# Attention stage: keys projected once and repeated through DRAM, 96-row operands, row maxima of batch 0 in the key bank

## What is computed

```python
B, S, D, H, HD = 32, 128, 128, 16, 8
q = split_heads(layernorm(x) @ Wq.T + bq)      # [B, H, S, HD]
k = split_heads(ctx @ Wk.T + bk)
v = split_heads(ctx @ Wv.T + bv)
scores = einsum('bhqd,bhkd->bhqk', q, k) / sqrt(HD)
attn = softmax(where(mask, finfo.min, scores), axis=-1)
x = x + tanh(g_xattn) * (merge(attn @ v) @ Wo.T + bo)
x = x + tanh(g_ffn) * ffn(layernorm(x))        # 8 experts, 512 hidden, thresholded softmax gate
```

## Time and profile before

| | us |
|---|---|
| median of 3 runs | 677.84 (677.28 to 678.39) |
| the profiled execution, its own time | 676.37 |
| its span, first to last instruction | 674.4 |
| PE busy | 635.5 (94%) |
| DVE busy | 544.5 (81%) |
| ACT busy | 433.8 (64%) |
| POOL busy | 185.6 (28%) |

### The profile page before, as it was taken

One profiled execution on the slowest core, in us unless ns is written; L12 is line 12 of the kernel. 1 busy time (PEld: TensorE's weight loads), 2 busy tenths in 40 slices (PEclk: granted clock), 3 DMA queues, 4 the chain that ended last, 5 costly groups with the idle time before them and its releaser, 6 DMA issues.

```text
span 674.4 us, 14486 instructions
## 1 busy us (share of the span) xinstructions
PE 635.5 (94%) x3964; PEld 483.3 (72%) x3964; DVE 544.5 (81%) x1085; ACT 433.8 (64%) x764; POOL 185.6 (28%) x240
## 2 busy tenths in 40 slices
PE   3999999999999999739999999999999999999998
PEld 2666666766666666427878878878788788787886
DVE  5778888998898888545888888888888888888886
ACT  3466666666666666417766766767667667666673
POOL 6224444444444442200121221221212212212121
PEclk9999999999999999958999999999999999999999
DMA  6544344444444444103112112111111111121110
GB/s 190 141 121 123 106 119 120 117 113 114 118 114 113 113 106 106 58 0 71 48 48 63 47 48 64 47 47 62 47 49 60 47 62 47 47 62 47 46 63 17
DMA packets 37402, 52.74 MB, mean 78 GB/s; under 512 B 9344, under 2 KB 20480, under 8 KB 37376
## 3 DMA queue, kind: packets, MB, share of 16 engines
q1 hardware_dynamic: 37376, 52.42, 28.4%
HBM read 26.58 MB, written 2.23 MB: 43 GB/s over the span
## 4 chain that ended last, share of the span: by engine, by line
PE 85%; DVE 6%; DMA 3%; SPq 2%; issue 2%; ACT 2%; POOL 0%; DVEq 0%; ACTq 0%; POOLq 0%
PE ps_h L1081 9%; PE ps_y L1061 9%; PE ps_y L1063 9%; PE ps_y L1062 9%; PE ps_h L1083 9%; PE ps_h L1082 9%; PE scores L1014 5%; PE scores L1015 4%; PE scores L1022 3%; PE scores L1023 3%; DVE neg_max L659 3%; PE heads L1033 3%; PE misc L902 2%; PE misc L903 2%; PE misc L904 2%; PE misc L888 2%
## 5 line engine op out<-in xcount | busy, mean ns | idle before, releaser
L632 ACT ACTIVATE h_sb<-ps_h,b_sb 128x512 f32<-128x512 f32 x256 | 175.9, 688 | 109.2 <-PE ps_h L1083 95.7
L846 DVE TENSOR_TENSOR h_low<-h_sb,h_high 128x512 fp32r<-128x512 f32 x256 | 164.4, 682 | 0.0
L842 DVE CAST h_high<-h_sb 128x512 fp32r<-128x512 f32 x128 | 98.8, 772 | 67.9 <-ACT h_sb L632 67.9
L528 POOL TENSOR_TENSOR yT<-yT,weighted 128x512 f32<-128x512 f32 x54 | 69.8, 1293 | 300.9 <-DVE weighted L834 300.9
L1081 PE MATMUL ps_h<-x_high,w_high 128*128 (+1 forms) x256 | 103.1, 403 | 1.7 <-ACT h_sb L632 1.6
L1061 PE MATMUL ps_y<-h_high,w_high 128*128 128x512 f32 x256 | 101.4, 396 | 0.8 <-DVE h_low L846 0.8
L1063 PE MATMUL ps_y<-h_high,w_low 128*128 128x512 f32 x256 | 101.3, 396 | 0.0
L1062 PE MATMUL ps_y<-h_low,w_high 128*128 128x512 f32 x256 | 101.2, 395 | 0.0
L1083 PE MATMUL ps_h<-x_high,w_low 128*128 (+1 forms) x256 | 100.6, 393 | 0.0
L1082 PE MATMUL ps_h<-x_low,w_high 128*128 (+1 forms) x256 | 100.2, 391 | 0.0
L659 DVE TENSOR_REDUCE neg_max<-scores 128x4 f32<-128x512 f32 x128 | 83.6, 686 | 9.8 <-PE scores L1023 9.2
(11 more groups left out here) (128 smaller groups left out, 1000.9 us busy)
## 6 DMA issues: line engine op xcount, KB each, us to landing
w_row<-w_scratch SPq DMA_DIRECT2D x64, 256.0 KB, 3.1
k_masked<-k_stack SPq DMA_DIRECT2D x64, 128.0 KB, 2.4
k_cur<-k_stack SPq DMA_DIRECT2D x16, 512.0 KB, 3.0
q_masked<-q_stack SPq DMA_DIRECT2D x64, 96.0 KB
w_raw<-in_w_ffn SPq DMA_DIRECT2D x16, 256.0 KB, 2.7
ctx_sb<-in_ctx SPq DMA_DIRECT2D x16, 128.0 KB, 2.1
out_y<-y_out SPq DMA_DIRECT2D x7, 256.0 KB, 2.3
probs<-in_wqk SPq DMA_DIRECT2D x2, 256.0 KB, 3.1
```

Source lines behind the costliest of these rows:

```text
L632: nc.scalar.activation(h_sb[:, j % HBUF, :], ps_h[:, j % 4, :], ACT.Gelu_apprx_tanh, bias=b1_sb[:, j:j + 1]).then_inc(h_done, 1)
L842: V.tensor_copy(h_high[:, j % HBUF, :], h_sb[:, j % HBUF, :]).then_inc(high_odd, 1)
L846: V.tensor_tensor(h_low[:, j % HBUF, :], h_sb[:, j % HBUF, :], h_high[:, j % HBUF, :].bitcast(F32), ALU.subtract).then_inc(low2_done, 1)
```

## The change

Keys are projected once: one matmul triple of 128 output rows (all 16 heads, 8 features each) instead of four of stacked rows. ACT adds the bias into k_high (rounded to float32r), DVE makes k_low. SP stores k_high twice and k_low once into a scratch tensor in DRAM, k_scratch, in the order of the repeats, and loads k_cur and the four blocks of k_masked from there. k_stack is gone. The spare rows are dropped: a head's block has 24 rows, a slab 96 (KROWS), and the query projection has 96 output rows. The two rows of ones stand once at rows 96 and 97 of k_cur, and the row maxima go to rows 96 and 97 of q_masked; `natural` contracts 96 rows, `transposed` 98.

The misc banks are dealt out anew: bank 0 holds k, x2T, the row maxima of batch 0, q01 and the inputs; bank 1 heads, merged, wo, gate and q23; bank 2 only v. The row maxima of batch 0 so share a bank with the key projections. The loop runs from -4 to NG + 1 instead of -3 to NG, most steps run one iteration further ahead, and the order inside the bodies of all five engines is new. The two q pairs have four `part` slabs of their own. The biases are gathered by 12 small DMAs on ACT's queue ahead of its first activation instead of two on SP's; DVE also sets the two rows of ones.

The core of the diff (the new bodies of SP and PE, the new steps of ACT and DVE; lines that take steps out or only move them are left out, as are the `settle` lines behind waits in PE's part and those inside loops):

```diff
-BANKS = [["p45", "inputs", "x2T", "p01"],
-         ["p67", "max0", "p23"],
-         ["v", "heads", "merged", "gate", "wo"]]
-AHEAD = {"p45": 1, "p67": 1, "v": 1, "inputs": 2, "x2T": -1, "max0": 1, "heads": 0,
-         "p01": 2, "merged": 0, "p23": 2, "gate": -1, "wo": 0}
-FIRST, LAST = -3, NG
-STEADY = (2, NG - 3)
+BANKS = [["k", "x2T", "max0", "q01", "inputs"],
+         ["heads", "merged", "wo", "gate", "q23"],
+         ["v"]]
+AHEAD = {"k": 2, "x2T": -2, "q01": 2, "inputs": 3,
+         "heads": -1, "merged": -1, "wo": -1, "max0": 1, "gate": -2, "q23": 2, "v": 2}
...
+k_dram = nc.dram_tensor("k_scratch", (NG, KROWS, SLABS * GT), F32)
...
+    store_v = k_dram[:].rearrange("g (r c d) (s t) -> g c r (d s) t", r=ROWS, c=3, t=GT)
+    def store(c, src, g, done):
+        sp.dma_start(of_group(store_v, g)[:, c].rearrange("g r p t -> (g r) p t"), src[:].bitcast(F32)).then_inc(done, 16)
+    def load(dst, rows, g):
+        return sp.dma_start(dst.rearrange("p s t -> p (s t)").bitcast(F32), of_group(k_dram[:], g)[:, rows, :].rearrange("g p x -> (g p) x"))
     def body(it):
+        if (g := group_at(it, 2)) is not None:
+            sp.wait_ge(k_high_done, g + 1)
+            store(0, k_high, g, high_stored)
+            store(2, k_high, g, high_stored)
+            misc_wait_read(sp, "k", g)
+            store(1, k_low, g, low_stored)
+        if (g := group_at(it, 1)) is not None:
+            sp.wait_ge(high_stored, g * 32 + 32)
+            sp.wait_ge(low_stored, g * 16 + 16)
+            if first(g):
+                sp.wait_ge(pad_done, 3)
+            else:
+                sp.wait_ge(scoresT_full[1], fill_of(g - 1, GB - 1, SLABS - 1))
+            load(k_cur[0:KROWS, :, :], slice(0, KROWS), g).then_inc(kcur_in, 16)
+            misc_wait_read(sp, "q01", g)
+            misc_wait_read(sp, "q23", g)
+            for r in range(ROWS):
+                rows = slice(3 * HD * r, 3 * HD * (r + 1))
+                sp.dma_start(q_masked[rows, r, :, :].bitcast(F32), q_stack[rows, :, :].bitcast(F32)).then_inc(qm_in, 16)
+            misc_wait_read(sp, "max0", g)
+            max_rows(0)
+        if (g := group_at(it, 2)) is not None and not first(g):
+            sp.wait_ge(masknxt_done, g)
+            sp.wait_ge(maskcur_done, g)
+            sp.dma_start(mask_words[:], of_group(mask_v, g)).then_inc(mask_in, 16)
+        if (g := group_at(it, 3)) is not None and not first(g):
+            misc_wait_full(sp, "inputs", g - 1)
+            sp.dma_start(ctx_sb[:], of_group(ctx_v, g).rearrange("g p b d -> (g p) b d")).then_inc(ctx_in, 16)
+        if (g := group_at(it, 2)) is not None:
+            if not first(g):
+                sp.wait_ge(wsplit_done, g)
+                sp.dma_start(w_raw[:], of_group(a["w_ffn"], g).rearrange("g p x -> (g p) x")).then_inc(w_in, 16)
+            sp.wait_ge(high_stored, g * 32 + 32)
+            sp.wait_ge(low_stored, g * 16 + 16)
+            if first(g):
+                sp.wait_ge(pad_done, 3)
             else:
                 sp.wait_ge(scoresN_full[1], fill_of(g - 1, GB - 1, SLABS - 1))
             for r in range(ROWS):
+                rows = slice(3 * HD * r, 3 * HD * (r + 1))
+                load(k_masked[rows, r, :, :], rows, g).then_inc(km_in, 16)
+        if (g := group_at(it, 1)) is not None:
+            sp.wait_ge(maxT1_done, g + 1)
+            max_rows(1)
...
+    bias_v = a["bqk"].rearrange("(r c d) (n s) -> n r c d s", r=ROWS, c=COMBOS, s=SLABS)
+    for r in range(ROWS):
+        rows = slice(3 * HD * r, 3 * HD * (r + 1))
+        act.dma_start(bk[4 * HD * r:4 * HD * (r + 1), :], bias_v[0, r, 0]).then_inc(bias_in, 16)
+        act.dma_start(bq[rows, :], bias_v[1, r, 0:3].rearrange("c d s -> (c d) s")).then_inc(bias_in, 16)
+        act.dma_start(low_rows[rows, :], a["low_rows"][4 * HD * r:4 * HD * r + 3 * HD, SLABS:]).then_inc(bias_in, 16)
...
+            misc_wait_full(act, "k", g)
+            wait_count(act, high_stored, g * 32)
+            nc.scalar.activation(k_high[:], misc[:, bank_of("k"), 0:GT], ACT.Identity, bias=bk[:]).then_inc(k_high_done, 1)
...
+            what = f"q{i}{i + 1}"
+            dve.wait_ge(part_done, g * SLABS + (i + 2))
+            if not first(g):
+                dve.wait_ge(qm_in, g * (ROWS * 16))
+                dve.wait_ge(scoresN_full[1], fill_of(g - 1, GB - 1, SLABS - 1))
+            for k in range(2):
+                ins = nc.vector.scalar_tensor_tensor(q_stack[0:KROWS, i + k, :], misc[0:KROWS, bank_of(what), k * GT:(k + 1) * GT],
+                                                     bq[0:KROWS, i + k:i + k + 1],
+                                                     part[0:KROWS, i + k, :].bitcast(F32), ALU.add, ALU.subtract)
+            ins.then_inc(misc_read[bank_of(what)], 1)
...
+            dve.wait_ge(k_high_done, g + 1)
+            wait_count(dve, low_stored, g * 16)
+            nc.vector.scalar_tensor_tensor(k_low[:], misc[:, bank_of("k"), 0:GT], bk[:],
+                                           k_high[:].bitcast(F32), ALU.add, ALU.subtract).then_inc(misc_read[bank_of("k")], 1)
         if (g := group_at(it, 2)) is not None:
-            stacks(0, g)
+            max_slab(g, 0, 0)
+            max_slab(g, 0, 1)
...
+                cols = slice(j * KROWS, (j + 1) * KROWS)
+                dst = misc[0:KROWS, k, (j - i) * GT:(j - i + 1) * GT]
+                mm(dst, wq_high[:, cols], src_h, start=True, stop=False)
+                mm(dst, wq_high[:, cols], src_l, start=False, stop=False)
+                ins = mm(dst, wq_low[:, cols], src_h, start=False, stop=True)
             ins.then_inc(misc_full[k], 1)
...
         if (g := group_at(it, 0)) is not None:
             transposed(g, 0, 2)
+        if (g := group_at(it, -1)) is not None:
+            misc_wait_free(pe, "heads", g)
+            pe.wait_ge(headsT_done, g + 1)
...
+            ins.then_inc(misc_full[bank_of("heads")], 1)
+        if (g := group_at(it, 0)) is not None:
+            pe.wait_ge(maxT1_done, g + 1)
+            misc_wait_read(pe, "v", g)
+            values(g, 0, 0)
+            transposed(g, 0, 3)
+        if (g := group_at(it, 2)) is not None:
+            if first(g):
+                pe.wait_ge(qk_w_done, 6)
+            misc_wait_read(pe, "inputs", g)
+            misc_wait_free(pe, "k", g)
+            dst = misc[:, bank_of("k"), 0:GT]
+            src_h, src_l = inT_high[:, 0:GT], inT_low[:, 0:GT]
+            mm(dst, wk_high[:], src_h, start=True, stop=False)
+            mm(dst, wk_high[:], src_l, start=False, stop=False)
+            mm(dst, wk_low[:], src_h, start=False, stop=True).then_inc(misc_full[bank_of("k")], 1)
+        if (g := group_at(it, 0)) is not None:
+            pe.wait_ge(max_in[1], g * 16 + 16)
+            transposed(g, 1, 0)
+        if (g := group_at(it, 1)) is not None:
+            misc_wait_read(pe, "q01", g)
+            misc_wait_read(pe, "q23", g)
+            pe.wait_ge(km_in, g * (ROWS * 16) + ROWS * 16)
+            pe.wait_ge(masknxt_done, g + 1)
+            natural(g, 0, 0)
+        if (g := group_at(it, -1)) is not None:
+            misc_wait_read(pe, "heads", g)
+            turn("merged", g, lambda b: merged[:, b * H:(b + 1) * H, :].rearrange("p h d -> p (h d)"))
+        if (g := group_at(it, 0)) is not None:
+            transposed(g, 1, 1)
+        if (g := group_at(it, 1)) is not None:
+            natural(g, 0, 1)
+        if (g := group_at(it, 0)) is not None:
+            transposed(g, 1, 2)
+        if (g := group_at(it, 1)) is not None:
+            natural(g, 0, 2)
+        if (g := group_at(it, 0)) is not None:
+            transposed(g, 1, 3)
+        if (g := group_at(it, 1)) is not None:
+            natural(g, 0, 3)
+        if (g := group_at(it, -1)) is not None:
+            if first(g):
+                pe.wait_ge(wts_in, N_WTS)
+            misc_wait_read(pe, "merged", g)
+            misc_wait_free(pe, "wo", g)
...
+            ins.then_inc(misc_full[bank_of("wo")], 1)
+        if (g := group_at(it, -2)) is not None:
+            pe.wait_ge(x2n_done, g * GB + GB)
+            turn("x2T", g, lambda b: x2n[:, b, :])
+        if (g := group_at(it, 1)) is not None:
+            natural(g, 1, 0)
+        if (g := group_at(it, 0)) is not None:
+            values(g, 0, 1)
+        if (g := group_at(it, 1)) is not None:
+            natural(g, 1, 1)
+            pe.wait_ge(max_done[0], g + 1)
+            misc_wait_free(pe, "max0", g)
+            nc.tensor.transpose(misc[0:2 * H, bank_of("max0"), 0:S], max_parts[:, 0, :].bitcast(F32), ident[:]).then_inc(misc_full[bank_of("max0")], 1)
+        if (g := group_at(it, -2)) is not None:
+            misc_wait_read(pe, "x2T", g)
+            misc_wait_free(pe, "gate", g)
...
+            ins.then_inc(misc_full[bank_of("gate")], 1)
+        if (g := group_at(it, 1)) is not None:
+            natural(g, 1, 2)
+        if (g := group_at(it, 2)) is not None:
+            queries(0, g)
+        if (g := group_at(it, 1)) is not None:
```

(53 more changed lines are left out.)

454 lines of the change are left out of this document (184 added, 270 removed).

## The result

The changed kernel takes 683.44 us (median of 5 runs, 681.06 to 688.87), the kernel before 677.28 us on the same chip. The ratio is 1.0107, 95% interval 1.0081 to 1.0133. The forecast was 668.6 us and faster. The time lies inside the range, the direction was wrong.

What follows compares the result with a forecast made beforehand. TensorE's queue was taken to bound the attention stage, afterwards SP's circle at 15.4 us a group. Middle -14.2, start +7, end -2 gave -9.2 us: 667.2 profiled, 668.6 us as median, range 660 to 685.

Steps and rivals of the forecast that it cites:

- SP's circle: Attention loop: SP's loads, landing of batch 1's maxima and PE's way back to transposed(g+1,1,3) take 15.4 us a group.
- the 14.2 us of the middle: First to sixteenth transposed row maxima: fifteen groups fall from 16.35 to 15.4 us, 14.2 us won.
- PE's price of the new order: Attention loop on TensorE: 14.15 us of matmuls plus changes of kind and the rest, a floor of 14.9 us a group.
- The maxima of batch 0 "cost nothing": Attention loop: their DMA issues 4.0 us behind transposed(g,1,3), PE wants it at 7.0, landing takes 2.32; no cost.
- Stores on four engines: Rival, chance 0.15: k stores to DRAM fill four of 16 DMA engines, a group takes 16.5 us, total 685.0 us.
- The queue rival: Rival, chance 0.12: in the attention loop SP's queue takes the place of PE, circle 16.2 us, total 680.6 us.
- The mask wait: Attention loop: mask_nxt, copied by POOL behind the first norm's power, comes 0.25 us before PE asks, the tightest buffer.
- The start: Before the first scores: stores queue behind x and cannot land before about 20 us; 7 us lost (4 to 8).
- The end: After the last group's scores: gate matmuls come behind the output matmuls, last maxima issue sooner; 2 us won (0 to 2.5).
- What would show it: Trace signs: 15.4 us a group, PE idle 0.5 us before transposed(1,0) with q_masked<-maxT as releaser, first scores at 26 to 29.
- the sign given for the four engines: Attention loop: PE's wait stands at transposed(0,0) and the stores land over 4 us after issue.
- one of the two signs of failure: The prediction fails if DVE or POOL turn up as releasers, or if the stores land before 18 us.

Runs made afterwards that it cites:

- the runs without late transfers: Changed kernel with two q_masked buffers, ctx behind k_cur, mask and w_raw behind the maxima of batch 1, stores for the first group only: 664.04 us, 0.9815 of before.
- the last version: Changed kernel with two q_masked buffers, mask and w_raw behind batch 1's maxima, ctx behind k_cur, stores spread over engines, three bias loads: 662.98 us, 0.9802 of before.

## Why the prediction was wrong

The step that failed is SP's circle: the forecast put it at 15.4 us and it took 16.15 us in the group shown (fifteen groups took 16.31 in the mean), so that the 14.2 us of the middle became 0.6. The circle was the right mechanism; its size was wrong, and the other terms below were wrong beside it.

- *PE's price of the new order, 14.9 us.* Mis-sized: the runs without late transfers give 15.43. One group of the last version adds up to 16 pairs 7.74, 15 projection matmuls 2.31, values 0.81, heads 2.16, the rest 2.41. Against the forecast's rows that is 0.38, 0.53, 0.19, 0.14 and 0.06 us more, 1.3 us over the price of the same matmuls in a row where 0.75 was allowed; that it is all changes of kind is argued, not shown. What failed in this term was reading 0.6 us of the kernel before as real waits; its run without maxima shows 0.16. The change saves TensorE 16.19 - 15.43 = 0.76 us a steady group, 11 us, if nothing else is late. The last version's middle is 245.29 - 230.03 = 15.3 us shorter than the middle before, near the 14.2 that the forecast gave the change alone.
- *SP's circle, 15.4 us, bounds 14.8 to 16.0.* The mechanism held, the size didn't. The way to the issue was right (9.63 us, forecast 9.6). That hides two errors: k_masked from DRAM was cheaper than its lower bound (1.81 us with gaps, forecast 2.4), and the waits and register work took 2.45 us where 1.3 to 1.6 were allowed. The landing took 2.73 instead of 2.32, the way from transposed(1,0) to (1,3) 3.8 instead of 3.44. These two are 0.77 us a group. The point from gain to loss, 16.02, was 0.6 us away.
- *The maxima of batch 0 "cost nothing".* Wrong. They were issued at 133.78, 4.3 us behind transposed(g,1,3), and released PE 3.06 us later instead of 2.32, at 136.84; PE stood 0.28 us. From there PE needs 8.6 us to the end of transposed(1,3), its next wait not counted, so this second circle is 4.3 + 3.1 + 8.6 = 16.0 us, nearly as long as the first.
- *Stores on four engines (0.15).* The mechanism is real: landing falls from 5.6 to 3.5 us for k_cur when the outer count changes alone. The rule of the Trainium skill ("DMA: Bandwidth & Descriptors", section "Why a DMA increments its semaphore by 16 and not by 1"), that the outermost counts of both sides set the number of engines, agrees with this case: with outer count 4 the share is 0.27, with outer count 32 a steady store lands in 2.1 us. The forecast priced it only as a circle through k_cur. Its real price is on whatever lands behind it, the 16 KB of maxima above all.
- *The queue rival (0.12), 680.6 us,* is the closest to what happened, by its place, its size of 16.2 a group and nearly its time. It wasn't alone: without the stores, or with a second q_masked buffer, the group stayed at 15.90 and 15.98 us. It had too small a chance because the circle was priced by durations of quiet rows, as if no row would grow by the traffic that the change adds. Reads from DRAM rose from 26.6 to 39.2 MB, writes from 2.2 to 8.5.
- *The mask wait* was not foreseen as a circle. The prediction named mask_nxt's cover of 0.25 us, not SP's wait for mask_cur. In the changed kernel it is hidden, since SP comes there at 134.83 us, 0.4 us after that copy ended.
- *The start, 7 us, measured 5.9.* The biases cost 1.55 us (first transpose 10.76 instead of 9.21, where "up to 1 us" was the bound). The stores landed at 21.94, where "not before about 20" was forecast; but x ahead of them, the forecast's reason, was worth 0.3 us only (k_masked at 21.77 without it), and their own four engines took the rest. First scores at 26.3, forecast 25.5 to 29.
- *The end, 2 won, measured 1.2 lost.* The gate matmuls did leave the place between the merged transpose and the output matmuls (295.46 to 295.99), and from that transpose to the logits it is 7.7 us instead of 9.4: 1.7 won. 1.36 of them are what the rows gave; some of the rest is luck, since the output matmuls ran at full clock (1.00 from 287 to 299 us) where before they ran at half (0.50 from 288 us on), 0.7 us instead of 1.2. But from the last row maxima to that transpose it is 18.0 us instead of 15.1, a path on which the prediction priced only the maxima's sooner issue. The traces divide these 2.9 us. 1.8 lie between the last pair of scores and the end of the last values (289.36 to 292.65 against 282.94 to 284.42): the output matmuls and other small blocks now stand there, and the values stand in two blocks with an exponential between them (290.02 and 291.95, before one block at 283.15). The other 1.1 lie ahead of the last pair, with a granted clock of 0.55 to 0.59 from 283 to 287 us, where it was 1.00 over the same stretch before. What each of the two alone would cost was not tried.
- *What would show it* worked: the window gives 16.3 and the releaser at transposed(1,0) is q_masked<-maxT, which with 15.4 would have been the forecast. It stood at transposed(0,0) too, the sign given for the four engines. VectorE, one of the two signs of failure, released TensorE once between 33 and 270 us, for 0.6 us; GpSimd never.

## What to carry to other kernels

When work is taken off the busiest engine and paid for in transfers, list every circle that comes back to the same buffer (single buffer, issue queue, landing, engine order) and price each landing with the new traffic ahead of it, not with the old rows. When several circles are about equally long, undoing them doesn't add up: against the changed kernel (1.0107) no stores alone gave 1.0007, a second buffer alone 0.9946, both 0.9958, a second buffer with the mask wait gone 1.0022, and only all three 0.9815. Before moving a transfer, look at the outermost count of both its sides; a change of row order, at no cost seen here, brought the store's landing to 2.1 us.

## What was not expected of the hardware

- A load issued on another queue still costs the issues on SP's: with k_cur issued by ScalarE's queue at 217.74 us the four q_masked issues took 0.84, 0.77, 0.88 and 1.12 us (3.75 with gaps) instead of 0.85, 0.77, 0.71 and 0.71 (3.19). The issue beside k_cur's own was not longer, the third and fourth were, when k_cur's issue had long ended; why was not tried.
- Issues of 24-row loads from DRAM are cheap, 0.30 to 0.33 us each, against 0.71 to 0.85 for the 24-row copies inside SBUF.
- A long wait of TensorE costs more than its own length. In the run with k_cur on ScalarE's queue it waited 2.82 us for the maxima until 55.69 us. Behind that the granted clock (last but two) was 0.61 for 4 us, so mostly at 1.2 GHz and not 2.4, and a mask matmul of 512 columns took 0.65 us (at 57.30) instead of 0.39 (at 61.35):

```profile
56.00:60.00 4.00, 4.00 (x19) 2.97 (x19) 1.79 (x7) 2.07 (x4) 1.87 (x4) 0.61 0.22 67
60.00:64.00 4.00, 4.00 (x35) 2.42 (x33) 2.03 (x5) 2.02 (x5) 0.61 (x1) 0.96 0.12 35
```
